# A cross-attention block on one core: proj's load and two copies behind the maxima's rows, fc's column sums split, four wide sums of exps, a bias sum moved

## What is computed

```python
residual = hidden_states
x = layer_norm(hidden_states, ln1_w, ln1_b)
q = x @ q_w + q_b            # split into 16 heads of 16
k = ctx @ k_w + k_b
v = ctx @ v_w + v_b
attn = softmax(where(mask, q @ k.T / 4, lowest))     # 64 x 64 per head and sequence
out = (attn @ v) @ cproj_w + cproj_b
hidden = out + residual
y = layer_norm(hidden, ln2_w, ln2_b)
y = gelu(y @ fc_w + fc_b)                            # width 1024
return hidden + y @ proj_w + proj_b
```

## Time and profile before

| | |
|---|---|
| three runs | 230.33, 232.28, 232.5 us |
| profiled execution | 232.38 us, its span 230.6 us |
| TensorE (PE) busy | 214.9 us, 93% of the span, 3520 products |
| VectorE (DVE) busy | 176.0 us, 76% |
| ScalarE (ACT) busy | 125.7 us, 55% |
| GpSimd (POOL) busy | 90.7 us, 39% |
| chain that ended last | PE 69%, DVE 11%, DMA 8%, issue 6% |
| mean granted TensorE clock | 0.985 of 2.4 GHz |

### The profile page before, as it was taken

One profiled execution on the slowest core, in us unless ns is written; L12 is line 12 of the kernel. 1 busy time (PEld: TensorE's weight loads), 2 busy tenths in 40 slices (PEclk: granted clock), 3 DMA queues, 4 the chain that ended last, 5 costly groups with the idle time before them and its releaser, 6 DMA issues.

```text
span 230.6 us, 8338 instructions
## 1 busy us (share of the span) xinstructions
PE 214.9 (93%) x3520; PEld 202.2 (88%) x3520; DVE 176.0 (76%) x378; ACT 125.7 (55%) x269; POOL 90.7 (39%) x101
## 2 busy tenths in 40 slices
PE   6978986878989999999999999999999999998995
PEld 6968976777979899999999999999999998897995
DVE  3678358866999796987979797979796779777571
ACT  3468357245923796169716972589248923651240
POOL 6345306528941195108621671248214611313300
PEclk9999798899999999999999999999999999999999
DMA  6958992950000483018500770079003900100101
GB/s 196 269 196 195 247 276 80 248 113 4 3 0 4 140 209 73 3 51 238 132 1 29 225 168 4 1 202 216 3 1 98 222 11 1 54 3 0 45 0 48
DMA packets 21980, 23.13 MB, mean 100 GB/s; under 512 B 1559, under 2 KB 20663, under 8 KB 21943
## 3 DMA queue, kind: packets, MB, share of 16 engines
q1 hardware_dynamic: 21008, 21.84, 37.3%
q10 hardware_dynamic: 934, 0.75, 1.1%
HBM read 7.62 MB, written 2.10 MB: 42 GB/s over the span
## 4 chain that ended last, share of the span: by engine, by line
PE 69%; DVE 11%; DMA 8%; issue 6%; ACT 2%; POOL 1%; SPq 1%; POOLq 0%; ACTq 0%
PE bank L1071 19%; PE bank L1072 16%; PE bank L1073 16%; PE bank L1149 6%; DMA stack_kq<-n_t 4%; DMA ctx_in<-in_ctx_t 4%; PE scores L1131 3%; PE scores L1101 3%; DVE recip L875 3%; PE bank L1088 3%; PE bank L1216 2%; DVE z L917 1%; POOL rs L560 1%; DVE mx L830 1%; DVE g_hi L892 1%
## 5 line engine op out<-in xcount | busy, mean ns | idle before, releaser
L1071 PE MATMUL bank<-proj_hi,g_hi 128*128 128x256 f32 x128 | 38.2, 299 | 2.4 <-DVE g_lo L894 2.4
L1071 PE MATMUL bank<-z_hi,fc_hi 128*128 128x256 f32 x128 | 37.5, 293 | 0.0
L1072 PE MATMUL bank<-z_hi,fc_lo 128*128 128x256 f32 x128 | 36.0, 281 | 0.0
L1072 PE MATMUL bank<-proj_hi,g_lo 128*128 128x256 f32 x128 | 36.0, 281 | 0.0
L1073 PE MATMUL bank<-proj_lo,g_hi 128*128 128x256 f32 x128 | 36.0, 281 | 0.0
L1073 PE MATMUL bank<-z_lo,fc_hi 128*128 128x256 f32 x128 | 35.9, 281 | 0.0
L875 DVE RECIPROCAL recip<-bank 128x256 f32<-128x256 f32 x16 | 28.0, 1751 | 5.1 <-PE bank L1149 5.1
L560 POOL TENSOR_TENSOR rs<-ve,power 128x1 f32<-128x1 f32 x16 | 9.9, 616 | 53.3 <-DVE ve L855 53.3
L631 ACT ACTIVATE fc_raw<-bank,fc_bias 128x256 f32<-128x256 f32 x64 | 26.7, 471 | 6.4 <-PE bank L1073 6.3
L1071 PEld LDWEIGHTS bank<-proj_hi,g_hi 128*128 128x128 f32 x128 | 24.1, 188 | 4.6 <-DVE g_lo L894 4.1
L830 DVE TENSOR_REDUCE mx<-scores 128x16 f32<-128x1024 f32 x16 | 19.5, 1220 | 10.3 <-PE scores L1101 10.3
(11 more groups left out here) (126 smaller groups left out, 586.9 us busy)
## 6 DMA issues: line engine op xcount, KB each, us to landing
stack_kq<-parts SPq DMA_DIRECT2D x48, 256.0 KB
x_in<-in_x SPq DMA_DIRECT2D x8, 256.0 KB, 3.3
ctx_in<-in_ctx_t SPq DMA_DIRECT2D x7, 256.0 KB, 3.4
out<-y SPq DMA_DIRECT2D x7, 256.0 KB, 2.1
fc_raw<-in_fc_w SPq DMA_DIRECT2D x1, 1024.0 KB, 9.3
proj_raw<-in_proj_w SPq DMA_DIRECT2D x1, 1024.0 KB, 9.8
ctx_in<-in_ctx_t ACTq DMA_DIRECT2D x1, 256.0 KB, 4.0
w_raw_q<-in_q_w SPq DMA_DIRECT2D x1, 256.0 KB, 4.7
```

Source lines behind the costliest of these rows:

```text
L1071: mm(out_ap, a_hi, b_hi, start=first, stop=False, skip_group_check=True)
L1072: mm(out_ap, a_lo, b_hi, start=False, stop=False, skip_group_check=True)
```

## The change

It has seven pieces; all but the fifth bear on the first steps alone:

1. On the sync engine the last set of group 1's copies (two of six) waits for `n_stacked[0]`, the landing of part 0's `n_t`, and proj's load for `n_stacked[1]`, that of part 1.
2. fc's column sums are made in two halves: 8 products behind group 1's v, 8 behind group 0's second score. They stood ahead of v. DVE's sum that reads them moves behind z's low part, and the product for cproj's bias no longer waits for it.
3. On TensorE `shift(b, 0)` moves ahead of group 2's q. One `keep_clock` of 14 ahead of the second turn of the maxima and one of 20 ahead of `project(b, 1, a)` go, one of 12 becomes 16.
4. `project(b, 1, a)` no longer waits for `q_left` 3; the small products behind it do.
5. In every `weigh` the 16 sums of 64 columns become 4 of 256 columns, ahead of the 16 products with v.
6. On POOL `x_and_bias(a)` moves from behind both row scales to between them.
7. The `keep_clock` of 24 in the first `full_step` becomes 16.

```diff
@@ stack_parts(g), sync engine
                 for k in range(PARTS):
+                    if g.c == 1 and k == PARTS - 1:
+                        sp.wait_ge(n_stacked[0], 16)
                     sp.wait_ge((k_lead, k_second, k_third)[k], g.count(1, 1))
...
@@ second_step(a, b), sync engine
                 stack_parts(a)
+                sp.wait_ge(n_stacked[1], 16)
                 load_w("proj", proj_raw, proj_w)
...
@@ second_step(a, b), GpSimd
                 row_scale(b, 0)
+                x_and_bias(a)
                 row_scale(b, 1)
-                x_and_bias(a)
                 pool.wait_ge(w_high["proj"], 1)
...
@@ second_step(a, b), VectorE
                 normal1(Group(0, 2))
-                dve.wait_ge(bias_summed, 2)
-                ve.tensor_tensor(fc_bias[:], bank7[:, 1, 0, 0:MB], col[:, COLS["fc_b"]:COLS["fc_b"] + MB],
-                                 ALU.add).then_inc(bias_ready, 1)
                 maxima(b, 0)
                 maxima(b, 1)
                 rest_of_z(Group(0, 2))
                 dve.wait_ge(bias_summed, 3)
+                ve.tensor_tensor(fc_bias[:], bank7[:, 1, 0, 0:MB], col[:, COLS["fc_b"]:COLS["fc_b"] + MB],
+                                 ALU.add).then_inc(bias_ready, 1)
                 dve.wait_ge(cb_loaded, 16)
...
@@ weigh(g, p), TensorE
                 wait(pe, o_made, g.count(2, p))
+                for i in range(4):
+                    mm(bank7[32 * i:32 * i + 32, 1, :, :], ones_bd[:].rearrange("p w d -> p (w d)"),
+                       probs[p][:, i:HP:4, :, :].rearrange("p h b q -> p h (b q)"),
+                       start=True, stop=True, skip_group_check=True)
                 for half in range(KC):
                     for b in range(2):
-                        cols_b = slice(S * b, S * b + S)
-                        for kind in range(2):
-                            for i in range(4):
-                                hp = 4 * half + i
-                                w = ones_bd[:] if kind else v_bd[g.slot][:, 2 * p + b, hp, :, :]
-                                last = mm(bank7[32 * i:32 * i + 32, kind, half, cols_b],
-                                          w.rearrange("p w d -> p (w d)"), probs[p][:, hp, b, :],
-                                          start=True, stop=True, skip_group_check=True)
+                        for i in range(4):
+                            hp = 4 * half + i
+                            last = mm(bank7[32 * i:32 * i + 32, 0, half, S * b:S * b + S],
+                                      v_bd[g.slot][:, 2 * p + b, hp, :, :].rearrange("p w d -> p (w d)"),
+                                      probs[p][:, hp, b, :], start=True, stop=True, skip_group_check=True)
                 last.then_inc(weighed, 1)
...
@@ second_step(a, b), TensorE
                 pe.wait_ge(bias_ready, 1)
-                column_sums(bank7[:, 1, 0, 0:MB], fc_raw, "ln2_b", range(MB)).then_inc(bias_summed, 1)
                 make_v(a, 0)
                 make_v(a, 1)
-                keep_clock(scores[:, 0, 0:P], 12)
+                column_sums(bank7[:, 1, 0, 0:MB], fc_raw, "ln2_b", range(MB // 2))
+                keep_clock(scores[:, 0, 0:P], 16)
...
                 score(b, 1)
+                column_sums(bank7[:, 1, 0, 0:MB], fc_raw, "ln2_b", range(MB // 2, MB)).then_inc(bias_summed, 1)
                 pe.wait_ge(w_loaded["c"], 16)
                 pe.wait_ge(vb_repeated, 1)
-                pe.wait_ge(bias_ready, 2)
...
                 pe.wait_ge(q_left, 2)
-                keep_clock(bank5[:, 0, 0:P], 14)
                 turn_maxima(b, 1)
                 keep_clock(bank5[:, 0, 0:P], 14)
+                shift(b, 0)
                 make_q(Group(0, 2))
-                shift(b, 0)
                 shift(b, 1)
...
                 make_v(Group(0, 2), 1)
+                project(b, 1, a)
                 pe.wait_ge(q_left, 3)
-                keep_clock(bank1[:, 0, 0:P], 20)
-                project(b, 1, a)
                 keep_clock(bank1[:, 0, 0:P], 14)
...
@@ full_step(a, b, c), TensorE
                 else:
-                    keep_clock(bank1[:, 0, 0:P], 24)
+                    keep_clock(bank1[:, 0, 0:P], 16)
```

## The result

The changed kernel takes 236.11 us (median of 8 runs, 233.62 to 237.53); the kernel before, beside it on the same chip, 231.80 (8 runs). Ratio 1.0149, 95% interval 1.0115 to 1.0183: slower by 1.5%. The forecast was 231.7 us, its range ended at 234.6.

A forecast was written before the change was run, and what follows sets the result against it. A chain of waits before the first fc product (57.17 us) bounds the kernel, then busy TensorE. Against 232.38 us: +0.6 (fc) - 0.98 (gap) - 0.3 (sums) = -0.7, so 231.7 us; range 227.8 to 234.6.

The forecast's parts named there:

- the gain of 4.2 us ahead of z: Start-up up to the second row scale on POOL: it ends at 49.2 instead of 53.42, 4.2 us gained.
- Landing of n_t: Copy of the maxima's rows for part 0: takes 3.45 us instead of 6.12, bounds 0 and 6.12.
- Shift at 33.7: TensorE's first shift of the maxima: starts at 33.7 us instead of 36.57.
- Second row scale done at 49.2: POOL's second row scale, ahead of the second z: ends at 49.2 us instead of 53.42.
- before's pause of 1.25: TensorE idle ahead of 20 small products before the second projection: goes with them, projection at 45.7 instead of 50.40.
- z waits for all of proj_lo: DVE's second z beside POOL's proj_lo: held for all of its 4.62 us, ending at 53.95.
- Clock behind z, 1.2 us: Shift and weighing between z and first fc product: run at 1.2 GHz, costing 1.2 us, bounds 0 and 3.4.
- the clock comes back late: Rival, from z's turn at 54.7 on: two stretches at 1.2 GHz, 2.7 us more, 234.4 us; chance 0.09.
- Gap of 0.98 closed: TensorE's wait for DVE's g_lo at 68.17 us: closes, gaining 0.98 us.
- Wide sums: Sums in each weighing, 4 of 256 columns for 16 of 64: gain 0.02 us each, 16 times, 0.3.
- The bound of a loss in the prediction: Wide sums in the weighings: a loss of 20 us if the four run one behind the other.
- the rival of +20 us: Rival on the weighings: the wide sums don't lie beside each other, +20, 252 us; chance 0.05.

The follow-up runs named there:

- e1: The changed kernel, unaltered, profiled once more for one execution: 238.05 us.
- d1: The changed kernel without the wait of proj's load for part 1's n_t: ratio to before 1.0004, median 236.57 us, profiled execution 232.69 us.
- e2: The kernel of d1 profiled once more for one execution: 232.43 us.
- b2: The kernel before with piece 5 (the wide sums) alone: 230.63 us, ratio to before 0.9919.
- a1: The changed kernel with piece 6 undone, xb behind both row scales again: 230.63 us, ratio to before 0.9898.
- b4: The kernel before with piece 6 alone, xb between the two row scales: 236.03 us, ratio to before 1.0156.
- a5: The changed kernel with proj_lo on POOL cut into four operations: ratio to before 0.9845 with 6 runs.
- e3: The same kernel as a5, measured once more: ratio to before 0.9954 with 12 runs.

## Why the prediction was wrong

Its sign was wrong, and the step that failed is the gain of 4.2 us ahead of z: the second row scale was to end at 49.2 instead of 53.42 and ended at 53.64, through low clocks and a pause on "issue" that the sum did not have. The term for the clock behind z was too small besides. Point by point:

- **Landing of n_t**: right, better than taken (2.0 us).
- **Shift at 33.7**: 36.42. Of these 2.7 us, 1.0 lies ahead of the first score, which starts at 26.31 for 25.3. The rest is the clock: I had counted one score at 1.2 GHz and let it come back; it stayed low until 29.8, and was low again in 33.3 to 36.6, where c's bias and the small products run behind the sums that the change put there (1.79 and 1.70 us for 1.13 and 0.9). In e1 it is low in 25.7 to 32.5, and the shift is at 36.01. In d1 and e2, with no low stretch there and the score at 26.00 and 26.05, the shift stands at 33.11 and 33.17.
- **Second row scale done at 49.2**: 53.64 and 55.22 in the changed kernel, 49.34 and 49.38 in d1 and e2. Beside the shift's delay of 2.7 it is the pause within the second weighing (1.73 and 2.17 us), of which DVE's second reciprocal waits for 1.52. The prediction had seen before's pause of 1.25, counted it as a loss that goes with its place, and never asked where the next would be; the changed kernel's is at the place of before's first one, of 0.32 us.
- **z waits for all of proj_lo**: right, 4.58 for the 4.62 forecast, and also 4.58 to 4.60 in each of the six other profiles that have piece 6, a whole proj_lo and no wait for z. The Trainium skill's "SBUF — State Buffer", SBUF: two separate sides, has the shared port pair locked for a whole instruction; the trace agrees.
- **Clock behind z, 1.2 us**: two stretches, as in the rival "the clock comes back late", and by its own test (the clock is at 1.2 GHz when the first `fc` product starts, at 62.28). z to `fc` takes 4.03 us instead of 2.36 (1.7 lost), `fc` to the product at 72.89 takes 10.61 with the gap gone, where 11.00 less 0.98 was due (0.6 lost): 2.3 in sum. That rival had 0.09, and even it left out the lost gain ahead of z.
- **Gap of 0.98 closed**: right. **Wide sums**: the size of a weighing right (1.02), but b2 gains 0.8%, and why stays open; the pauses that went with fewer instructions may be a part. The bound of a loss in the prediction took 0.97 us for two fp32 products of 256 columns from the earlier trace rows, whose row has 1.13 us; only the rival of +20 us hung on it.
- **Sum**: +5.1 at `fc`, -0.98 + 0.6 to 72.89, +0.4 over the rest gives the +5.15 of the profiled execution; forecast +0.6, -0.98, -0.3.

In d1 and e2 each step came as forecast (`fc` at 57.98 and 57.82 for 57.8, and 232.69 and 232.43 us for 231.7): the chain was read rightly for an execution without the low clock at 26 to 37 us and the pause, and in part by luck, since there the first score starts 0.7 us later than taken and then runs at 2.4 GHz. The changed kernel's two profiles are not like that, nor are most of d1's timed executions. And the cost of piece 6 was priced rightly at z and then set off against a gain that wasn't there: a1 shows that piece 6 decides the sign, and b4 that alone it makes before as slow as the changed kernel is. Without piece 6 the change gains 1.0% (a1), and piece 5 alone gives 0.8% (b2). What pieces 2 to 4 and 7 are worth was not tried by itself.

## What to carry to other kernels

Before you move a small operation on GpSimd out from between a VectorE operation and a long GpSimd one, see what then stands next to it: a short neighbour shields, and cutting the long one into pieces bounds the wait by a piece. Idle time of TensorE is paid twice where the clock falls behind it; small products that bridge it took back 2 us here, and a forecast should carry the low stretches of the whole start-up, not of one place. A pause on "issue" moves with the count of instructions and with what the DMA queues hold; a load put later to free one small copy can land on it.

## What the runs showed that was not expected

- The pause on "issue" lies at a fixed count of TensorE's products (471 or 472 in 13 profiles, 126 more for the second one in four), and ends 2.2 to 2.9 us behind an instruction packet: for example packets at 38.08, 39.13, 43.06 and 44.85 us, ends at 40.91, 41.66, 45.47 and 47.32. That it is the loading of instructions is inferred from this; no row says so. Why it needs that long after the packet is open.
- Even a VectorE operation of 128x16 is held by GpSimd: 0.75 instead of 0.17 us.
- The same start-up, proj's wait aside, runs with the clock low from 26 us on in six of twelve profiles and without in the other six; the second row scale ends at 52.25 to 55.22 in the first, at 49.34 to 51.89 in the second.
- Two profiles of one kernel differ by 1.6 us at one place (the changed kernel's row scale, 53.64 and 55.22 us), and two sets of runs of one kernel by 1.9 us in their medians (a5 and e3, 228.94 and 230.84 us).
